# Cross-attention and expert FFN on one Trainium2 core: every moved probability tile turned by VectorE, four work banks, remainders and slot picks on GpSimd

## The chip, the cores and the metric

The kernel runs on one core of one Trainium2 chip. The metric is device time in microseconds (us) of one execution; a kernel's time is the median of several executions. The engines are TensorE (PE, with PEld for its weight loads), VectorE (DVE), ScalarE (ACT), GpSimd (POOL) and SyncE (SP), which here only issues transfers.

## The reference, cut to what matters

16 batches of 256 tokens, width 256, with a context of 256 rows of width 192; 16 heads of 64; then a top-2 router over 8 experts with a capacity of 640 rows each.

```python
x = x + attention(layernorm(x), ctx)       # w_q 256x1024, w_k and w_v 192x1024, w_o 1024x256
  sim = einsum('bhid,bhjd->bhij', q, k) * 64 ** -0.5
  out = einsum('bhij,bhjd->bhid', softmax(sim), v)
x = x + ffn(layernorm(x))                  # gates, top 2 of 8, capacity, gelu(buf @ w1 + b1) @ w2 + b2
```

All of it is in 32-bit floats. Most products are made of three: each operand is split into a rounded head (`qh`, `kh`, `ah`) and its remainder (`ql`, `kl`, `al`), and the product of two remainders is left out.

## The kernel before, in words

The attention part is cut into 64 periods, four to a batch; a period m handles four heads ("units" 0 to 3, two pairs `cc`). `timeline()` writes one list of stages, and each engine walks that list and runs its own stages in that order, so the order on every engine is fixed by hand. Semaphores join them. In period m:

- PE: `scores(m)` into banks 0 to 3, one bank for each unit; `pv(m-2)` (probabilities by values); `q(m+1)`, `k(m+1)`, `v(m)`; and by batch the output projection `o` (twice), the transposes `xt` and `x2t`, `logits` and `pos`.
- DVE: `max0` to `max3` (row maxima), `a_norm` (attended values by the inverse row sums), `inv` (reciprocals and their turn), the remainders `a_lo`, `q_lo`, `k_lo`, and router work.
- ACT: `exp0` to `exp3`, the heads `q_hi`, `k_hi`, `a_hi`, `v_sb`, and `copy2`, `copy3`.
- POOL: context splits (`ctx`), inverse roots, the residual with its bias, and `scatter` (four indirect transfers into the slot table).
- SP: `inv_out(m-1)`, `inv_in(m-1)`, `lift(m)`, `move(m)`, and once a batch `traffic`, which stores a batch and loads the next `x` and context.

The probabilities of a unit are 256x256 and have to be transposed before `pv`. Outside `MOVED` (periods 6 to 61, 56 of the 64) PE does it: four 128x128 transposes for each unit (`turn`), and ACT copies the result out of the bank. In `MOVED` PE turns units 2 and 3 alone (`by_pe`). Units 0 and 1 go another way: DVE turns every 32x32 square in place (`square0`, `square1`, L1279), `lift` writes the 512 KB of both units to memory (`squares`, L485), and `move` (L492) reads them back with the squares in transposed places, in four transfers, one for each group of 32 partitions.

`move(m)` waits on SP until `lift(m)` has landed. The inverse row sums make a like round: `inv_out` (L466) writes 128 partitions of 32 values to the table `inverses`, `inv_in` (L475) waits until that has landed and reads them back spread over 64 partitions, twice. All of this is one queue in one order:

```python
sp.wait_ge(sem("inv_out"), 16 * (m + 1))                # inv_in(m)
sp.wait_ge(sem("square"), 2 * (m - MOVED[0] + 1))       # lift(m)
sp.wait_ge(sem("lifted"), 16 * (m - MOVED[0] + 1))      # move(m)
sp.dma_start(inv_table[m % 2].rearrange("j (a i) -> a j i", a=GROUPS), invturned[:, m % 2, :])
```

`pv(m)` waits for `moved`. Products of `xt`, `q`, `k`, `v`, `pv`, `o`, `x2t` and `pos` take banks 5, 6, 7 in turn (`WORK_BANKS = 3`); each waits until the product three places before has been read. Bank 4 holds a turn of PE or the logits.

Of the kernel before, what the change touches and what calls it, by code (L numbers as in the profile page):

```python
# [19 lines left out]
F32 = mybir.dt.float32  # L20
# [44 lines left out]
MOVED = range(6, PERIODS - 2)  # L65
SQ = 32
# [3 lines left out]
def by_pe(m):  # L70

    return (2, 3) if m in MOVED else (0, 1, 2, 3)

# [11 lines left out]
def timeline():  # L85
# [12 lines left out]
    for m in range(1, PERIODS - 2):  # L98
# [4 lines left out]
        out += [("scores", m)] + ([("pv", m - 2)] if m >= 2 else [])  # L103
        out += [("logits", b - 2)] if r == 3 and 2 <= b else []
        if four:
            out += [("q", m + 1), ("turn0", m - 1), ("k", m + 1), ("turn1", m - 1), ("v", m), ("turn2", m - 1)]
        else:
            out += [("q", m + 1), ("turn2", m - 1), ("k", m + 1), ("turn3", m - 1), ("v", m)]
# [12 lines left out]
        out += steps("exp0 exp1", m) + ([("a_hi", m - 2)] if m >= 2 else []) + [("q_hi", m + 1)]  # L121
        if four:
            out += [("copy0", m - 1), ("exp2", m), ("k_hi", m + 1), ("copy1", m - 1), ("exp3", m), ("copy2", m - 1),
                    ("v_sb", m)]
        else:
            out += [("copy2", m - 1), ("k_hi", m + 1), ("exp2", m), ("copy3", m - 1), ("exp3", m), ("v_sb", m)]
# [9 lines left out]
        out += ([("a_norm", m - 2)] if m >= 2 else []) + [("inv", m - 1)]  # L136
        out += [("slot", b - 3)] if r == 2 and 3 <= b else []
        out += [("bias", b - 2)] if r == 3 and 2 <= b else []
        out += [("ln1_stats", 1)] if m == 1 else []
        out += ([("a_lo", m - 2)] if m >= 2 else []) + [("q_lo", m + 1)]  # L140
        out += [("square0", m)] if m in MOVED else []
        out += [("k_lo", m + 1)]
        out += [("square1", m)] if m in MOVED else []
        if r == 0:
            out += steps("shift compare rank gate", b - 3) if 3 <= b else []
            out += [("ln1", b + 1)] if 1 <= b < B - 1 else []
# [3 lines left out]
        if r == 2:  # L150
            out += steps("ln1 xt_lo", 1) if b == 0 else []
            out += [("ln2", b - 2)] if 2 <= b else []
            out += [("ln1_stats", b + 2)] if b + 2 < B else []
            out += [("keys", b - 3)] if 3 <= b else []
            out += [("x2add", ST * (b - 1))] if 1 <= b else []
        out += [("pick", b - 3)] if r == 3 and 3 <= b else []
# [5 lines left out]
                5: [("vsplit", 3)]}.get(m, [])  # L162
        out += [("scatter", b - 4)] if r == 0 and 4 <= b else []
# [5 lines left out]
        out += [("load_ctx", 3)] if m == 2 else []  # L169
        out += steps("inv_out inv_in", m - 1) + (steps("lift move", m) if m in MOVED else [])  # L170
        out += {2: steps("clear", 0), 3: steps("clear", 1), 4: steps("clear", 2)}.get(m, [])
        out += [("traffic", b - 2)] if r == 1 and 2 <= b else []
# [4 lines left out]
    out += [("scores", m), ("pv", m - 2), ("q", z), ("turn2", m - 1), ("k", z), ("turn3", m - 1), ("v", m),  # L177
# [5 lines left out]
    out += [*steps("exp0 exp1", m), ("q_hi", z), ("a_hi", m - 2), ("copy2", m - 1), ("k_hi", z), ("exp2", m),  # L183
            ("copy3", m - 1), ("exp3", m), ("v_sb", m), ("x2t_sb", c), ("w_hi", 0), ("w_hi", 1),
# [5 lines left out]
    out += [*steps("max0 max1 max2 max3", m), ("inv", m - 1), ("slot", c - 1), ("a_norm", m - 2), ("q_lo", z),  # L190
            ("a_lo", m - 2), ("k_lo", z), ("ln2", c), *steps("keys pick", c - 1), ("x2add", ST * d), ("inv", m),
# [16 lines left out]
def w_piece(w, cut):  # L208
# [6 lines left out]
WORK_BANKS = 3  # L215
# [5 lines left out]
APART = {**{("logits", b): 4 for b in range(B - 3)}, ("x2t", B - 2): 2, ("logits", B - 2): 3, ("pos", B - 2): 4, ("logits", B - 1): 4}  # L221
# [7 lines left out]
WORK_READ = {"xt": "xt_lo", "q": "q_lo", "k": "k_lo", "v": "v_sb", "pv": "a_lo", "o": "x2", "x2t": "x2t_sb",  # L229
             "logits": "biased", "pos": "slots"}  # L230


def build(nc, x, ctxt, wq, wk, wv, wo, bo, rw, rb, w1, b1, w2, b2, out):
    es = ExitStack()
    with es:
# [12 lines left out]
        square_table = nc.dram_tensor("squares", [2, P, 2 * ST * S], F32, kind="Internal").ap()  # L248
# [15 lines left out]
        invrows = sb(rest, "invrows", [2, S])  # L264
        xth, xtl = (sb(rest, n, [2, DC, S], F32R) for n in ("xth", "xtl"))
        c0 = sb(rest, "c0", [2, S])
        c1 = sb(rest, "c1", [2, S])
# [73 lines left out]
        def prob_pair(m):  # L341
            return flat(prob[:, m % 2, 0:2, :, :, :])

        def probt_pair(m):
            return flat(probt[:, m % 2, 0:2, :, :])
# [54 lines left out]
        def _(sp):  # L400
# [6 lines left out]
            def load_ctx(b):  # L407
                if b >= 2:
                    sp.wait_ge(sem("ctx"), b - 1)
                cols = slice(b * S, (b + 1) * S)  # L410
                sp.dma_start(c0[:, b % 2, :], ctxt[0:P, cols]).then_inc(sem(f"ctx_in{b % 2}"), 16)
                for h in range(2):
                    sp.dma_start(c1[h * HD:(h + 1) * HD, b % 2, :], ctxt[P:CD, cols])\
                      .then_inc(sem(f"ctx_in{b % 2}"), 16)
# [38 lines left out]
            load_ctx(2)  # L453

# [25 lines left out]
            def lift(m):  # L480
# [81 lines left out]
        def _(pool):  # L562
# [20 lines left out]
            def ctx(b):  # L583

                p = b % 2
                pool.wait_ge(sem(f"ctx_in{p}"), 48 * (b // 2 + 1))
# [3 lines left out]
                link(pool.tensor_copy(c1s[0:HD, p, :], c1[0:HD, p, :]))  # L590
                link(pool.tensor_copy(c1t[HD:P, :], c1[HD:P, p, :]))
                link(pool.tensor_copy(c0h[:, p, :], c0[:, p, :]))
                link(pool.tensor_tensor(c1s[HD:P, p, :], c1[HD:P, p, :], c1t[HD:P, :].bitcast(F32), ALU.subtract))
                link_as("ctx", pool.tensor_tensor(c0l[:, p, :], c0[:, p, :], c0h[:, p, :].bitcast(F32),
                                                  ALU.subtract))

            def inverse_root(which, n):
# [13 lines left out]
                link_as(f"{which}_rstd", pool.tensor_tensor(root, root, newton[:, :], ALU.mult))  # L611

# [44 lines left out]
            def slots(b):  # L657
# [6 lines left out]
                if b < B - 4:  # L664
                    pool.wait_ge(sem("q"), PER_B * (b + 4) + 2)
# [8 lines left out]
            for stage, n in TIMELINE:  # L674
# [9 lines left out]
                if stage in ("ln1_root", "ln2_root"):  # L684
                    inverse_root(stage[:3], n)
                if stage == "vsplit":
# [27 lines left out]
        def _(pe):  # L714
            work = {w: n for n, w in enumerate(WORKS)}

            def bank(stage, n):

                if stage == "logits" and n < B - 3:
                    pe.wait_ge(sem("probt"), turns_to(PER_B * (n + 2) + 1, UNITS - 1))  # L720
                    return psum[:, APART[stage, n], :]
# [4 lines left out]
                at = work[stage, n]  # L726
                if at >= WORK_BANKS:
                    s, m = WORKS[at - WORK_BANKS]
                    pe.wait_ge(sem(WORK_READ[s]), m + 1)
                return psum[:, 5 + at % WORK_BANKS, :]  # L730

# [74 lines left out]
            def turn(m, u):  # L806

                if u == 0 and m >= 1:
                    pe.wait_ge(sem("probt"), turns_to(m - 1, 3))
                if u in (1, 2) and m + 1 < PERIODS:  # L810
                    pe.wait_ge(sem("exp"), UNITS * (m + 1) + u)
                if u == 3:
                    pe.wait_ge(sem("probt"), turns_to(m, 0))
                    if m % PER_B == 2 and 2 <= m // PER_B < B - 1:
                        pe.wait_ge(sem("biased"), m // PER_B - 1)
# [7 lines left out]
            def pv(m):  # L823
# [7 lines left out]
                for cc in range(2):  # L831
                    for kb in range(ST):
                        for h in range(2):
                            cols = slice((2 * (c + cc) + h) * HD, (2 * (c + cc) + h + 1) * HD)
                            if m in MOVED and cc == 0:
                                p = probt_pair(m).rearrange("p (a u k q i) -> p u k q a i", a=GROUPS, u=2, k=ST, q=ST)[:, h, kb]
# [5 lines left out]
            def o(n, chunks=range(PAIRS)):  # L842

                b, t = divmod(n, ST)
                dst = bank("o", n) if chunks[0] == 0 else psum[:, 5 + work["o", n] % WORK_BANKS, :]
# [160 lines left out]
        def _(act):  # L1006
            copy = lambda dst, src, **kw: act.activation(dst, src, ACT.Copy, **kw)  # L1007
            def work_bank(stage, n):
                if (stage, n) in APART:
                    return psum[:, APART[stage, n], :]  # L1010
                return psum[:, 5 + WORKS.index((stage, n)) % WORK_BANKS, :]
# [38 lines left out]
            def exps(m, u):  # L1050
# [5 lines left out]
                if m >= 2 and u in by_pe(m - 2):  # L1056
                    act.wait_ge(sem("turn"), turns_to(m - 2, u))
                elif m >= 2:
                    act.wait_ge(sem(f"moved{m % 2}"), 16 * moves_to(m - 2))
                for qb in range(ST):  # L1060
                    into, out_of = prob[:, m % 2, u, :, qb, :], psum[:, u, qb * S:(qb + 1) * S]
                    if m in MOVED and u not in by_pe(m):
                        into = prob_pair(m).rearrange("p (g u k q j) -> p u q k g j", g=GROUPS, u=2, k=ST, q=ST)[:, u, qb]
# [17 lines left out]
            def pv(m):  # L1081
# [6 lines left out]
                copy(ah[:, b % 2, c:c + 2, :], work_bank("pv", m).rearrange("p (c s) -> p c s", c=2))\  # L1088
# [97 lines left out]
        def _(dve):  # L1186
# [7 lines left out]
            def work_bank(stage, n):  # L1194
                if (stage, n) in APART:
                    return psum[:, APART[stage, n], :]
                return psum[:, 5 + WORKS.index((stage, n)) % WORK_BANKS, :]
# [71 lines left out]
            def a_norm(m):  # L1269
# [3 lines left out]
                at = work_bank("pv", m).rearrange("p (c s) -> p c s", c=2)  # L1273
                dve.tensor_tensor(at, at, invrows[:, :, :], ALU.mult).then_inc(sem("a_norm"), 1)  # L1274

            def square(m, u):
# [278 lines left out]
```

## Time and profile before

| | us |
|---|---|
| median of 3 runs | 954.8 (954.76 to 957.25) |
| the profiled execution | 957.82 |
| its span | 956.1 |
| PE busy | 918.1 (96%) |
| DVE busy | 739.8 (77%) |
| ACT busy | 573.8 (60%) |
| POOL busy | 280.2 (29%) |
| DMA moved | 133.29 MB, 139 GB/s on average |

The span runs from the first to the last instruction of the profiled execution; its time is 1.7 us longer. A busy engine is not always the one that sets the end: the waits in front of it say so. SP has no busy time in the page; what it does is in its own timeline.

### The profile page before, as it was taken

Reading aid. Unit: us, or ns where it says so; the run is one execution under the profiler, and the core shown is the slowest. Engines: PE = TensorE matmul, PEld = TensorE weight load, DVE = VectorE, ACT = ScalarE, POOL = GpSimd, SP = SyncE. Lnnn points to the kernel's source line nnn. Section 1 sums busy time; section 2 is a strip of 40 time slices with the busy share of each in tenths; the row PEclk is TensorE's granted clock in tenths of the full one; section 3 lists DMA queues with packets and bytes.
Section 4 is the critical chain, followed back from the end, with each engine's and each line's share of the span. In section 5 each row is a group of like instructions: output and inputs, shape, how many; then the busy total and the mean of one; then the engine's idle time right before and its main releaser. Section 6 shows DMA issues by size and latency. Waiting matters only on the chain.

```text
span 956.1 us, 22462 instructions
## 1 busy us (share of the span) xinstructions
PE 918.1 (96%) x7916; PEld 821.0 (86%) x7916; DVE 739.8 (77%) x1745; ACT 573.8 (60%) x1600; POOL 280.2 (29%) x441
## 2 busy tenths in 40 slices
PE   7999999999999999999999999999889999999995
PEld 7878888888888888888888888888689999999995
DVE  5757778888888888888888888877777877678762
ACT  5877766667667666766766677676534433334420
POOL 5541112314233231323223132302533223322233
PEclk9999999999999999999999999999899999999999
DMA  8462535445455445455444445444345765645422
GB/s 239 143 205 91 163 123 163 162 152 168 146 157 158 148 157 164 136 172 164 139 156 161 146 130 170 136 134 136 121 133 99 149 145 123 135 84 98 112 29 27
DMA packets 152991, 133.29 MB, mean 139 GB/s; under 512 B 62140, under 2 KB 141610, under 8 KB 152752
## 3 DMA queue, kind: packets, MB, share of 16 engines
q1 hardware_dynamic: 144048, 122.87, 42.9%
q0 software_dynamic: 8832, 8.98, 5.4%
q8 instruction: 64, 1.05, 0.5%
q14 instruction: 47, 0.39, 0.1%
HBM read 82.15 MB, written 54.61 MB: 143 GB/s over the span
## 4 chain that ended last, share of the span: by engine, by line
PE 70%; DVE 11%; ACT 10%; issue 4%; DMA 3%; POOL 0%; SPq 0%; POOLq 0%; ACTq 0%; DVEq 0%
PE psum L734 20%; PE psum L839 9%; PE psum L996 9%; PE psum L855 9%; PE psum L980 8%; PE psum L801 7%; ACT prob L1067 6%; PE psum L819 5%; DVE negmax L1255 3%; DVE hidl L1201 2%; DVE bufl L1201 1%; ACT probt L1007 1%; DVE hidh L1488 1%; PE psum L879 1%; DVE psum L1274 1%
## 5 line engine op out<-in xcount | busy, mean ns | idle before, releaser
L1067 ACT ACTIVATE prob<-psum,negmax 128x256 f32<-128x256 f32 x512 | 238.0, 481 | 79.5 <-DVE negmax L1255 79.4
L1255 DVE TENSOR_REDUCE negmax<-psum 128x2 f32<-128x512 f32 x256 | 160.4, 682 | 29.7 <-PE psum L801 29.7
L1173 ACT ACTIVATE hid<-psum,b1t 128x640 f32<-128x640 f32 x64 | 50.9, 795 | 126.6 <-PE psum L980 125.0
L839 PE MATMUL psum<-probt,v 128*64 128x256 f32 x1024 | 124.6, 385 | 0.0
L707 POOL DMA_INDIRECT out_rows<-y,rowi x40 | 66.3, 1658 | 160.8 <-DVE y L1498 154.2
L1067 ACT ACTIVATION_READ_ACCUMULATOR prob<-psum,negmax 128x1 f32 x512 | 109.5, 214 | 0.0
L839 PEld LDWEIGHTS psum<-probt,v 128*64 128x64 f32 x1024 | 67.8, 136 | 36.4 <-issue 0.3
L668 POOL DMA_INDIRECT slot_table<-row,picki x64 | 66.8, 1044 | 96.9 <-PE psum L734 61.2
L996 PE MATMUL psum<-w2h,hidh 128*128 128x256 f32 x320 | 91.4, 286 | 2.9 <-DVE y L1498 1.5
L801 PE MATMUL psum<-kh,qh 64*128 64x256 f32 x512 | 82.5, 316 | 11.1 <-ACT prob L1067 8.9
L996 PE MATMUL psum<-w2l,hidh 128*128 128x256 f32 x320 | 90.5, 283 | 0.0
L996 PE MATMUL psum<-w2h,hidl 128*128 128x256 f32 x320 | 90.5, 283 | 0.0
L1007 ACT ACTIVATE probt<-psum 128x512 f32<-128x512 f32 x144 | 87.3, 609 | 4.4 <-PE psum L819 4.4
L819 PE MATMUL psum<-ident,prob 128*128 128x128 f32 x576 | 87.1, 276 | 2.7 <-ACT prob L1067 2.7
L734 PE MATMUL psum<-xth,wqh 128*128 128x256 f32 x256 | 78.9, 308 | 0.5 <-DVE xtl L1201 0.5
L1279 DVE STREAM_TRANSPOSE prob<-prob 128x512 f32<-128x512 f32 x112 | 78.6, 702 | 0.0
L855 PE MATMUL psum<-woh,ah 128*128 128x256 f32 x256 | 72.9, 285 | 1.6 <-DVE al L1201 1.6
L606 POOL TENSOR_SCALAR shifted<-ln_mean_var 128x2 f32<-128x2 f32 x32 | 7.1, 223 | 225.0 <-issue 182.7
L801 PE MATMUL psum<-kl,qh 64*128 64x256 f32 x512 | 72.9, 278 | 0.0
L801 PEld LDWEIGHTS psum<-kh,qh 64*128 64x128 f32 x512 | 48.8, 185 | 27.9 <-ACT prob L1067 13.3
L801 PE MATMUL psum<-kh,ql 64*128 64x256 f32 x512 | 72.8, 277 | 0.0
L855 PE MATMUL psum<-wol,ah 128*128 128x256 f32 x256 | 72.4, 283 | 0.0
(199 smaller groups left out, 2704.6 us busy)
## 6 DMA issues: line engine op xcount, KB each, us to landing
squares<-prob SPq DMA_DIRECT2D x56, 512.0 KB
probt<-squares SPq DMA_DIRECT2D x224, 128.0 KB, 2.8
invrows<-inverses SPq DMA_DIRECT2D x128, 128.0 KB
w1r<-in_w SPq DMA_DIRECT2D x8, 1024.0 KB
w2r<-in_w SPq DMA_DIRECT2D x8, 1024.0 KB, 9.1
slot_table<-blank SPq DMA_DIRECT2D x8, 662.5 KB, 6.5
blocks<-slot_table SPq DMA_DIRECT2D x56, 80.0 KB
xin<-in_x SPq DMA_DIRECT2D x16, 256.0 KB, 3.5
```

The lines of the kernel that those rows point to most:

```text
L668: pool.indirect_dma_start(out=table, out_offset=bass.IndirectOffsetOnAxis(ap=picki[:, b % 3, k, t:t + 1], axis=0), in_=row[:, b % 3, t, :] ...
L734: mm = pe.matmul(dst, lhs, rhs, start=(j == 0), stop=(j == len(terms) - 1))
L801: mm = pe.matmul(psum[:, 2 * cc + h, qb * S:(qb + 1) * S], a[r, m % 2, cc, cols], w[r, m % 2, cc, :], start=(j == 0), stop=(j == len(terms ...
L819: mm = pe.transpose(psum[:, TURN_BANK[u], kb * S + qb * P:kb * S + (qb + 1) * P], prob[:, m % 2, u, kb, qb, :], ident[:, :])
L839: mm = pe.matmul(dst[h * HD:(h + 1) * HD, cc * S:(cc + 1) * S], v[:, b % 2, kb, cols], p, start=(kb == 0), stop=(kb == ST - 1))
L855: mm = pe.matmul(dst[:, 0:D], a[:, b % 2, c, tt], w[:, c, :], start=(c == 0 and j == 0), stop=(c == PAIRS - 1 and j == 2))
L980: mm = pe.matmul(dst, lhs, rhs, start=(n == 0), stop=(n == len(terms) - 1))
L996: mm = pe.matmul(dst, a[:, j, ss], w[:, j, :], start=(j == 0 and m == 0), stop=(j == HC - 1 and m == 2))
L1007: copy = lambda dst, src, **kw: act.activation(dst, src, ACT.Copy, **kw)
L1067: last = act.activation(into, out_of, ACT.Exp, bias=negmax[:, m % 2, u, qb:qb + 1], accum_out=total[:, m % 2, u, qb:qb + 1])
L1255: dve.tensor_reduce(negmax[:, m % 2, u, :], psum[:, u, :].rearrange("p (q s) -> p q s", q=ST), AX.X, ALU.max, negate=True).then_inc(sem("m ...
L1279: dve.transpose(at, at).then_inc(sem("square"), 1)
```

## The change

1. In `MOVED`, `by_pe` is empty: PE turns nothing and ACT copies nothing. DVE turns the squares of all four units, in two instructions of 128x1024 (pairs of units) where there were two of 128x512.
2. `lift` writes all four units, 1 MB. `move` reads them back in four transfers again, now one for each group `a` of 32 source rows, each into all 128 partitions.
3. Bank 4 joins the work banks from period 6 on until period 62 (`places()`), also for the logits.
4. `pv(m-2)` comes after `q` and `k` in PE's period. `a_norm` writes to a new SBUF tile `attended` instead of back to its bank, and comes after `q_lo`, `square0`, `k_lo`; `a_hi` and `a_lo` read `attended`.
5. To POOL go `a_lo` of periods 4 to 59, `ln1` of batches 2 to 15, and the last steps of the slot picks (`pick_`, ranked by a subtraction); DVE keeps the two reductions (`extremes`).
6. On SP, `traffic` comes between `inv_out` and `inv_in`. The context tiles `c0`, `c1` have one buffer, and `scatter` starts after a `k` instead of a `q`.

```diff
 def by_pe(m):
-    return (2, 3) if m in MOVED else (0, 1, 2, 3)
+    return () if m in MOVED else (0, 1, 2, 3)
...
-            out += [("q", m + 1), ("turn2", m - 1), ("k", m + 1), ("turn3", m - 1), ("v", m)]
+            out += [("scores", m)] + ([("logits", b - 2)] if r == 3 and 2 <= b else [])
+            out += [("q", m + 1), ("k", m + 1), ("pv", m - 2), ("v", m)]
...
-            out += [("copy2", m - 1), ("k_hi", m + 1), ("exp2", m), ("copy3", m - 1), ("exp3", m), ("v_sb", m)]
+            out += [*steps("exp0 exp1", m), ("q_hi", m + 1), ("exp2", m), ("k_hi", m + 1), ("exp3", m),
+                    ("a_hi", m - 2), ("v_sb", m)]
...
+            out += [("inv", m - 1)] + ([("slot", b - 3)] if r == 2 and 3 <= b else [])
+            out += [("bias", b - 2)] if r == 3 and 2 <= b else []
+            out += [("q_lo", m + 1), ("square0", m), ("k_lo", m + 1), ("a_norm", m - 2)]
         out += [("square1", m)] if m in MOVED else []
...
-        out += steps("inv_out inv_in", m - 1) + (steps("lift move", m) if m in MOVED else [])
+        out += [("inv_out", m - 1)] + ([("traffic", b - 2)] if r == 1 and 2 <= b else [])
+        out += [("inv_in", m - 1)] + (steps("lift move", m) if m in MOVED else [])
...
-                sp.dma_start(square_table[m % 2], prob_pair(m)).then_inc(sem("lifted"), 16)
+                sp.dma_start(square_table[m % 2], prob_all(m)).then_inc(sem("lifted"), 16)
...
-                for g in range(GROUPS):
-                    sp.dma_start(probt_pair(m)[g * SQ:(g + 1) * SQ, :].rearrange("j (a c) -> j a c", a=GROUPS),
-                                 square_table[m % 2].rearrange("(a j) (g c) -> g j a c", a=GROUPS, g=GROUPS)[g])\
+                for a in range(GROUPS):
+                    sp.dma_start(probt_all(m).rearrange("p (a c) -> p a c", a=GROUPS)[:, a, :],
+                                 square_table[m % 2].rearrange("(a j) (g c) -> a g j c", a=GROUPS, g=GROUPS)[a])\
                       .then_inc(sem(f"moved{m % 2}"), 16)
...
+            def a_lo(m):
+                b, c = divmod(2 * m, PAIRS)
+                pool.wait_ge(sem("a_hi"), m + 1)
...
+                pool.tensor_tensor(al[:, b % 2, c:c + 2, :], attended[:, :, :],
+                                   ah[:, b % 2, c:c + 2, :].bitcast(F32), ALU.subtract).then_inc(sem("a_lo"), 1)
...
-                dve.tensor_tensor(at, at, invrows[:, :, :], ALU.mult).then_inc(sem("a_norm"), 1)
...
+                dve.tensor_tensor(attended[:, :, :], work_bank("pv", m).rearrange("p (c s) -> p c s", c=2),
+                                  invrows[:, :, :], ALU.mult).then_inc(sem("a_norm"), 1)
+
+            def square(m, pair):
+
+                dve.wait_ge(sem("exp"), UNITS * m + 2 * pair + 2)
+                at = prob_all(m).rearrange("p (g v c) -> p v g c", g=GROUPS, v=2)[:, pair]
                 dve.transpose(at, at).then_inc(sem("square"), 1)
```

## Rows read from the trace of the kernel before

**Rows 1.** The page: span and busy time of each engine.
```profile
span 956.1 us, 22462 instructions
PE 918.1 (96%) x7916; PEld 821.0 (86%) x7916; DVE 739.8 (77%) x1745; ACT 573.8 (60%) x1600; POOL 280.2 (29%) x441
```

**Rows 2.** One batch: us, busy of PE, PEld, DVE, ACT, POOL; clock, DMA share, GB/s.
```profile
389.06:431.10 42.04, 41.30 (x380) 35.58 (x379) 35.35 (x93) 29.11 (x92) 11.68 (x23) 1.00 0.48 154
```

**Rows 3.** The chain that ended last, 389 to 431 us: start, us, what.
```profile
391.32 0.44 PE psum L819 x4
```

**Rows 4.** Groups by shape, window 389.06 to 431.10: busy, mean ns, idle before.
```profile
L1279 DVE STREAM_TRANSPOSE prob<-prob 128x512 f32<-128x512 f32 x8 | 5.6, 702 | 0.0
...
L1007 ACT ACTIVATE probt<-psum 128x512 f32<-128x512 f32 x8 | 4.8, 601 | 0.0
...
L1201 DVE TENSOR_TENSOR al<-psum,ah 128x512 fp32r<-128x512 f32 x4 | 2.8, 692 | 1.1 <-ACT ah L1007 1.1
```

**Rows 5.** Groups by shape, whole span: the nearest rows for new shapes.
```profile
L1217 DVE TENSOR_SCALAR turning<-xin,ln_mean_var,ln_rstd 128x256 f32<-128x256 f32 x32 | 12.0, 418 | 2.6 <-POOL ln_rstd L611 2.3 <-issue 0.3
L1470 DVE STREAM_TRANSPOSE turned<-blocks 128x640 f32<-128x640 f32 x14 | 11.6, 834 | 0.0
...
L594 POOL TENSOR_TENSOR c0l<-c,c0h 128x256 fp32r<-128x256 f32 x16 | 12.2, 762 | 1.3
...
L617 POOL TENSOR_TENSOR wol<-wo_raw,woh 128x1024 fp32r<-128x1024 f32 x2 | 4.8, 2378 | 0.2
```

**Rows 6.** SP's timeline over one batch: start, us, issue.
```profile
389.06 1.75 SPq L492 DMA_DIRECT2D probt<-squares  x4
...
399.88 1.74 SPq L492 DMA_DIRECT2D probt<-squares  x4
401.66 0.57 SPq L466 DMA_DIRECT2D inverses<-invturned  x1
404.05 1.24 SPq L475 DMA_DIRECT2D invrows<-inverses  x2
405.39 0.54 SPq L485 DMA_DIRECT2D squares<-prob  x1
408.86 1.73 SPq L492 DMA_DIRECT2D probt<-squares  x4
...
413.85 0.58 SPq L466 DMA_DIRECT2D inverses<-invturned  x1
416.26 1.28 SPq L475 DMA_DIRECT2D invrows<-inverses  x2
...
421.35 1.75 SPq L492 DMA_DIRECT2D probt<-squares  x4
...
430.56 1.73 SPq L492 DMA_DIRECT2D probt<-squares  x4
```

**Rows 7.** SP's waits, window 78 to 663: us in total, times, longest.
```profile
SPq L492 <- DMA squares<-prob: 174.1, 56, 4.8
SPq L475 <- DMA inverses<-invturned: 78.6, 46, 2.5
SPq L466 <- DVE invturned L1267: 13.9, 12, 3.0
SPq L485 <- DVE prob L1279: 11.1, 17, 1.3
```

**Rows 8.** DMA, window 637.20 to 638.90, one `lift` alone: packets, share.
```profile
DMA packets 144, 0.52 MB, mean 308 GB/s; under 512 B 16, under 2 KB 16, under 8 KB 144
...
q1 hardware_dynamic: 144, 0.52, 76.2%
```

**Rows 9.** DMA, window 611.90 to 612.50, one `inv_out` alone.
```profile
DMA packets 132, 0.02 MB, mean 27 GB/s; under 512 B 132, under 2 KB 132, under 8 KB 132
...
q1 hardware_dynamic: 132, 0.02, 17.9%
```

**Rows 10.** DMA, window 401.75 to 402.75, in the middle of a `move`.
```profile
q1 hardware_dynamic: 299, 0.27, 88.0%
```

More of the change, by code:

```diff
@@ L65 @@
 MOVED = range(6, PERIODS - 2)
+POOL_REST = range(PER_B, PERIODS - 4)
 SQ = 32
@@ L135, in timeline @@
         out += ([("split_lo", 5)] if m == 1 else []) + steps("max2 max3", m)
[L136 to L142, printed above, removed]
+        if four:
+            out += ([("a_norm", m - 2)] if m >= 2 else []) + [("inv", m - 1)]
+            out += [("ln1_stats", 1)] if m == 1 else []
+            out += ([("a_lo", m - 2)] if 0 <= m - 2 < POOL_REST[0] else []) + [("q_lo", m + 1)]
+            out += [("square0", m)] if m in MOVED else []
+            out += [("k_lo", m + 1)]
+        else:
+            out += [("inv", m - 1)] + ([("slot", b - 3)] if r == 2 and 3 <= b else [])
+            out += [("bias", b - 2)] if r == 3 and 2 <= b else []
+            out += [("q_lo", m + 1), ("square0", m), ("k_lo", m + 1), ("a_norm", m - 2)]
         out += [("square1", m)] if m in MOVED else []
@@ L162, in timeline @@
                 5: [("vsplit", 3)]}.get(m, [])
+        out += [("ln1", b + 1)] if r == 0 and 1 <= b < B - 1 else []
         out += [("scatter", b - 4)] if r == 0 and 4 <= b else []
@@ L228, with places @@
 WORKS = [w for w in WORKS if w not in APART]
-WORK_READ = {"xt": "xt_lo", "q": "q_lo", "k": "k_lo", "v": "v_sb", "pv": "a_lo", "o": "x2", "x2t": "x2t_sb",
+WORK_READ = {"xt": "xt_lo", "q": "q_lo", "k": "k_lo", "v": "v_sb", "pv": "a_norm", "o": "x2", "x2t": "x2t_sb",
              "logits": "biased", "pos": "slots"}
+def places():
+    banks, last, found = [5, 6, 7], {}, {}
+    for stage, n in TIMELINE:
+        work = stage.removesuffix("_most"), n
+        if (stage, n) == ("turn0", PERIODS - 2):
+            banks.remove(4)
+            found[stage, n] = 4, last[4]
+        if work in WORKS and work not in found:
+            at = banks.pop(0)
+            banks.append(at)
+            found[work] = at, last.get(at)
+            last[at] = work
+        if (stage, n) == ("turn3", MOVED[0] - 1):
+            banks.append(4)
+    return found
+PLACES = places()
 def build(nc, x, ctxt, wq, wk, wv, wo, bo, rw, rb, w1, b1, w2, b2, out):
@@ L611, in inverse_root, with ln1, pick_ @@
                 link_as(f"{which}_rstd", pool.tensor_tensor(root, root, newton[:, :], ALU.mult))
+            def ln1(b):
+                pool.wait_ge(sem("xt"), b)
+                if b >= XRING:
+                    pool.wait_ge(sem("logits"), b - XRING + 1)
+                for t in range(ST):
+                    last = pool.tensor_scalar(xn[:, t, :], xin[:, b % XRING, t, :], mean_var["ln1"][:, t, 0:1],
+                                              rstd["ln1"][:, t:t + 1], ALU.subtract, ALU.mult)
+                last.then_inc(sem("ln1"), 1)
+            def a_lo(m):
+                b, c = divmod(2 * m, PAIRS)
+                pool.wait_ge(sem("a_hi"), m + 1)
+                if m == POOL_REST[0]:
+                    pool.wait_ge(sem("a_lo"), m)
+                    pool.wait_ge(sem("table_clear"), 16 * NE)
+                    pool.wait_ge(sem("spare_clear"), 16)
+                pool.tensor_tensor(al[:, b % 2, c:c + 2, :], attended[:, :, :],
+                                   ah[:, b % 2, c:c + 2, :].bitcast(F32), ALU.subtract).then_inc(sem("a_lo"), 1)
+            def pick_(b):
+                pool.wait_ge(sem("extremes"), b + 1)
+                if b >= 3:
+                    pool.wait_ge(sem(f"scatter{b % 3}"), 16 * 2 * ST * (b // 3))
+                pool.tensor_scalar(pick[:, 0, :], pick[:, 0, :], BIG, None, ALU.add)
+                link(pool.tensor_scalar(pick[:, 1, :], pick[:, 1, :], -1.0, None, ALU.add))
+                link(pool.tensor_tensor(same[:, 0, :], pick[:, 1, :], pick[:, 0, :], ALU.subtract))
+                link(pool.tensor_scalar(same[:, 0, :], same[:, 0, :], 0.0, BIG, ALU.is_le, ALU.mult))
+                link(pool.tensor_tensor(pick[:, 1, :], pick[:, 1, :], same[:, 0, :], ALU.add))
+                pool.tensor_copy(picki[:, b % 3, :, :], pick[:, :, :]).then_inc(sem("picks"), 1)
             def vsplit(w):
@@ L685, in _ @@
                     inverse_root(stage[:3], n)
+                if stage == "ln1" and n >= 2:
+                    ln1(n)
+                if stage == "a_lo" and n in POOL_REST:
+                    a_lo(n)
+                if stage == "pick" and n < B - 4:
+                    pick_(n)
                 if stage == "vsplit":
@@ L725, in bank @@
                     return psum[:, APART[stage, n], :]
[L726 to L730, printed above, removed]
+                at, user = PLACES[stage, n]
+                if user:
+                    pe.wait_ge(sem(WORK_READ[user[0]]), user[1] + 1)
+                elif at == 4:
+                    pe.wait_ge(sem("probt"), turns_to(MOVED[0] - 1, UNITS - 1))
+                return psum[:, at, :]
             def products(dst, terms):
@@ L1453, in _ @@
             for stage, n in TIMELINE:
-                if stage in steps:
+                if stage in steps and not (stage == "ln1" and n >= 2 or stage == "a_lo" and n in POOL_REST
+                                               or stage == "pick" and n < B - 4):
                     steps[stage](n)
```

121 lines of the change are left out of this document (60 added, 61 removed).

## The prediction

> **What bounds the kernel now.** I read the page first, then one batch by stretches, then the chain, then SP. The page gives PE 96% of the span and DVE 77% [rows 1]. The stretch of one batch says where that matters: PE is busy 41.30 of 42.04 us, DVE 35.35, ACT 29.11, POOL 11.68, at the full granted clock [rows 2]. The chain runs through PE for nearly all of the batch, the turns of PE included, 0.44 us each [rows 3]. So far PE is the bound.
>
> A second loop is nearly as long, and no busy column shows it. SP works in strict order: `move` waits for `lift` to land, and `inv_in` for `inv_out`. The starts of five successive `move`s lie 10.82, 8.98, 12.49 and 9.21 us apart, 41.50 in all, for a batch of 42.04 [rows 6]; the 12.49 has `traffic` in it. Of its waits between 78 and 663 us, 174.1 us are for a `lift` to land and 78.6 us for an `inv_out`. DVE kept SP waiting for 13.9 and 11.1 us in all, 25 us over 14 batches, or 1.8 us a batch [rows 7]. That is all the slack SP has. Any microsecond the change puts between one `move` and the next, beyond 1.8 a batch, lengthens the kernel, whatever PE gives back.
>
> **The change part by part.**
>
> *PE and ACT.* Eight turns of PE go from each batch: 8 x 0.44 = 3.5 us [rows 3]. With the 0.74 us in which PE is idle now [rows 2], a batch could fall to 37.8 us. ACT loses eight copies, 4.8 us [rows 4]; it is not the bound.
>
> *DVE.* There is no 128x1024 transpose in the trace. 128x512 takes 0.702 us [rows 4], 128x640 takes 0.834 [rows 5], so 1.03 ns for each further element and 1.23 us for 1024; its bounds are 0.83 and 1.40 (two of 0.702). I take 1.23: +8 x 0.53 = +4.2 us a batch (+1.0 to +5.6). It gives up four `a_lo` of 0.69 (2.8 us) [rows 4], two tensor_scalar of 0.42 (0.8 us) [rows 5], and the tail of a pick, five small instructions that I put at 0.5 to 1 us, by the 0.2 to 0.4 of the small rows. DVE ends near 35.2 us a batch, about what it has.
>
> *POOL.* A 128x512 subtraction lies between 0.76 (128x256) and 2.38 us (128x1024) [rows 5]; on the line between, 1.30. Four of them, two `ln1` instructions of 0.4 to 0.8 and a pick make about 8 us: 20 of 42. Hidden behind PE or DVE, with `a_lo` a whole period ahead of the next `a_norm`; if that cover failed it would cost DVE up to 1.3 us a period.
>
> *Banks, orders, context.* Four banks, `pv` after `k`, and one context buffer move waits, not work. Cost nothing: `pv(m)` now comes some 3 us later in its period, which covers late transfers; the context load still has about three periods.
>
> *lift.* A `lift` alone is 144 packets: 128 of data and 16 small ones that signal [rows 8]. 76.2% of 1.7 us on 16 engines is 20.7 us, so 161 ns for each 4 KB packet, eight to an engine. Twice the bytes: +8 x 0.161 = +1.3 us until it lands, for each period. `move` waits for it, so all of it is on SP's path: +5.2 us a batch.
>
> *move.* This decides. Before, both sides of each of its four transfers have 32 rows outermost. Now the destination has 128 partitions outermost, and the source `(g j) c` has 4 blocks of 32 rows. The trace has one transfer with such a pair of sides, in the other direction: `inv_out`, 128 partitions to a table walked 4 x 32. It shows 132 packets, 128 of data and 4 that signal, where a `lift` has 16 [rows 8, 9]. Its share is 17.9% of 0.6 us on 16 engines, 1.72 us or 13 ns a packet, and `lift` fills three quarters of the engines' time where this fills a sixth. I read that as four engines instead of 16, one for each block of the outer 4, and expect the same when the 4 is on the source side. The profile doesn't show which engines; as all `inv_out`s and `move`s would be of one kind, I take the same four.
>
> The price then: 4 transfers x 128 packets of 2 KB on 4 engines are 128 packets for each. A packet of 2 KB lies on the line between 13 ns (128 B) and 161 ns (4 KB): 85 ns, bounds 80 (half of 161) and 94 (two of a `move` of now, 88.0% x 1 us x 16 / 299 packets = 47 ns) [rows 8 to 10]. 128 x 85 ns = 10.8 us (10.2 to 12.0).
>
> The Trainium skill, DMA: Bandwidth & Descriptors, section "Why a DMA increments its semaphore by 16 and not by 1", says that a transfer takes the largest number of engines up to 16 that divides the outermost size of both sides, and the lowest-numbered ones. By that rule the new `move` takes four, always the same, and the sum is the one below; were the count set by the destination alone, it would be the 16-engine rival. The trace agrees for a destination of 4 (the four signals of rows 9); for a source of 4 no run here shows it.
>
> *inv_out behind move.* Now it is issued 1.78 us after `move` starts, and `inv_in` at +4.17 (404.05 - 399.88) [rows 6]. Of that, move's own data are 512 x 47 ns / 16 engines at 88% [rows 10], 1.7 us; 2.5 us are the start, inv_out's own data and its landing. With 10.8 us of data on four engines, and `inv_out` queued behind them on the same four, `inv_in` starts at +13.3: 9.1 more in each of the three periods without `traffic`. In the period with it, `inv_in` started at +7.4 (416.26 - 408.86); it is +5.9 there, and I take 1 (0 to 2) for traffic's data, which now lie in front of the lift.
>
> *The sum.* 41.5 + 3 x 9.1 + 5.9 + 1 + 5.2 = 80.9 us for four periods; less the waits on DVE, which vanish (1.8), 79.1. That is 37 us more than 42.04, over 56 moved periods or 14 batches: +519 us. The profiled execution takes 957.8, so 1477; the median is 3 us lower than that execution: 1474, say **1470 us**. A packet of 80 or 94 ns moves it by -36 or +65 us, the term for `traffic` by 14 either way, the bounds of the lift by little. I put this case's own range at 1400 to 1540.
>
> **Rivals.**
>
> 1. *All 16 engines carry the move, SP still the bound (0.24).* Then a `move` has 32 packets of 85 ns for each engine instead of 32 of 47: +1.2 us. `inv_out`'s signal comes 0.6 to 1.1 later, +2.4 us for three periods; `traffic` between saves 1.6 in the fourth; `lift` +5.2. 41.5 + 2.4 - 1.6 + 5.2 = 47.5 a batch, 45.7 less the slack of 1.8: +3.7 to +5.5, +52 to +77 us, so 1005 to 1030; 1015 is its price, and some 980 if transfers overlap better than that. For it: only the source has the 4. Against it: the pair of sides is that of `inv_out` mirrored.
>
> 2. *The other sign: SP's loop isn't lengthened and PE is paid (0.13).* Place: SP between `lift` and the next `lift`. It decides if the doubled transfers add less than 1.8 us a batch, where I count at least 5.2 for `lift` alone. Then PE's 37.8 us holds, -4.2 x 14 = -59 us at most, some of it lost to DVE at 93% of that: 900 to 920. For it: DMA is busy 48% on average [rows 2], and `pv` has 3 us more grace. Against it: average share says nothing of a queue that waits for each landing.
>
> 3. *DVE becomes the bound in its own order (0.05, with what is not foreseen).* Its 35.2 us is in order behind waits on `pv`, ACT and now POOL; 1.3 us for each period would bring 42 again: 950 to 975.
>
> **How the numbers follow.** The four-engine move gets 0.58. Its mechanism rests on one row of the mirrored kind, which is why it isn't more. The predicted time is its own, 1470. The range must reach to the 16-engine case, so it is 980 to 1545: 0.55 of the first, 0.23 of the second. Differences of 0.3% are about what a measurement of this kernel can tell from none. Faster 0.13 (rival 2); same 0.03 (part of rival 3); slower 0.84.
>
> **What would show it.** In the profile after: `move` starts some 19 to 20 us apart; a single `move` transfer with 4 signalling packets, 132 in place of 144; DMA share near a quarter for 10 us of each period; `inv_in` 13 us behind `move`; PE and DVE both half idle, PE's wait on `probt` before `pv`. Right for 16 engines: intervals near 11.5 us, 144 packets a transfer. Wrong on both counts: PE still 98% busy in a batch of 38 us. If the four transfers used four different sets of engines, they would run side by side in 3 us and the result would be rival 1's. No turn of PE (L819) should be left between 90 and 650 us, and DVE's two transposes should take 1.2 us each.

## The result: 1491 us, 56% slower

| | us |
|---|---|
| before, median of 4 runs | 955.65 (954.76 to 957.25) |
| changed, median of 4 runs | 1491.01 (1486.35 to 1493.18) |
| ratio | 1.559 (95%: 1.555 to 1.564) |

The page of the changed kernel: busy time and share of each engine, then the granted clock in 40 slices, and the chain that ended last.

```profile
span 1491.4 us, 21278 instructions
PE 987.3 (66%) x7468; PEld 835.7 (56%) x7468; DVE 744.5 (50%) x1601; ACT 516.7 (35%) x1488; POOL 401.2 (27%) x597
...
PEclk9997777888777787777888787778777779999999
...
DMA 55%; PE 22%; SPq 8%; DVE 8%; issue 3%; ACT 2%; POOLq 0%; POOL 0%; ACTq 0%; DVEq 0%
DMA inverses<-invturned 29%; DMA probt<-squares 14%; DMA squares<-prob 12%; PE psum L1056 6%; PE psum L1040 6%; PE psum L899 5%; SPq L517 5%; SPq L500 3%; DVE negmax L1316 2%; PE psum L792 2%; PE psum L859 1%; DVE hidl L1262 1%; ACT prob L1128 1%; DVE prob L1343 1%; DVE bufl L1262 1%
```

No engine is busy for more than two thirds of the span, where PE had 96% [rows 1]. The chain is 55% DMA, and its first entry is a table of 16 KB, the inverse sums. SP's timeline over two periods (start, us, issue) shows why:

```profile
608.66 2.45 SPq L517 DMA_DIRECT2D probt<-squares  x4
611.15 1.48 SPq L491 DMA_DIRECT2D inverses<-invturned  x1
...
622.23 1.26 SPq L500 DMA_DIRECT2D invrows<-inverses  x2
623.60 0.54 SPq L510 DMA_DIRECT2D squares<-prob  x1
628.42 2.44 SPq L517 DMA_DIRECT2D probt<-squares  x4
630.91 1.53 SPq L491 DMA_DIRECT2D inverses<-invturned  x1
641.18 1.25 SPq L500 DMA_DIRECT2D invrows<-inverses  x2
...
647.38 2.50 SPq L517 DMA_DIRECT2D probt<-squares  x4
```

The `move`s start 19.8 and 19.0 us apart, where they had 9 to 12.5 [rows 6]. `inv_in` starts 13.6 us behind `move` with `traffic` and 12.8 without; it was 4.2 without. The DMA packets from the start of a `move` to `inv_in` (628.42 to 641.20):

```profile
DMA packets 661, 1.08 MB, mean 85 GB/s; under 512 B 148, under 2 KB 148, under 8 KB 660
```

148 small packets are the 128 of `inv_out` and 20 that signal: four for each of five transfers. `inv_out` alone had 4 and `lift` 16 [rows 8, 9]. In the middle of the `move` (631.00 to 639.50):

```profile
DMA packets 432, 0.86 MB, mean 101 GB/s; under 512 B 12, under 2 KB 12, under 8 KB 432
...
q1 hardware_dynamic: 432, 0.86, 26.1%
```

For 8.5 us the share is 26.1%, four engines of 16 with nothing between packets: 26.1% x 8.5 x 16 / 420 data packets = 84.5 ns each. Had the four transfers used different sets of engines, they would have run side by side and the share would have been up to four times that. Which four engines they are, no run shows.

SP's waits between the first and the last `move` (window 83 to 1194: us, times, longest), to be read against [rows 7], which cover the same 56 `move`s:

```profile
SPq L500 <- DMA inverses<-invturned: 420.9, 55, 11.2
SPq L517 <- DMA squares<-prob: 237.6, 56, 6.0
SPq L491 <- DVE invturned L1328: 15.1, 17, 1.6
```

The wait for the inverses, and the 29% that the chain gives them, is not the time of 16 KB: `inv_out` is issued at 630.91, and the `move` in front of it has landed only at 640.85.

### The profile page after: what moved, and what is told of

Same layout as the page of the kernel before. It is cut to its first block, busy times and chain, and to the rows that moved or that the text cites. A ratio compares the mean times of both kernels' runs of the same rounds, so it can differ in the third digit from the quotient of the medians.

```text
span 1491.4 us, 21278 instructions
## 1 busy us (share of the span) xinstructions
PE 987.3 (66%) x7468; PEld 835.7 (56%) x7468; DVE 744.5 (50%) x1601; ACT 516.7 (35%) x1488; POOL 401.2 (27%) x597
## 4 chain that ended last, share of the span: by engine, by line
DMA 55%; PE 22%; SPq 8%; DVE 8%; issue 3%; ACT 2%; POOLq 0%; POOL 0%; ACTq 0%; DVEq 0%
DMA inverses<-invturned 29%; DMA probt<-squares 14%; DMA squares<-prob 12%; PE psum L1056 6%; PE psum L1040 6%; PE psum L899 5%; SPq L517 5%; SPq L500 3%; DVE negmax L1316 2%; PE psum L792 2%; PE psum L859 1%; DVE hidl L1262 1%; ACT prob L1128 1%; DVE prob L1343 1%; DVE bufl L1262 1%
## 5 line engine op out<-in xcount | busy, mean ns | idle before, releaser
L899 PE MATMUL psum<-probt,v 128*64 128x256 f32 x1024 | 218.1, 599 | 476.6 <-DMA probt<-squares 476.6
L899 PEld LDWEIGHTS psum<-probt,v 128*64 128x64 f32 x1024 | 115.9, 212 | 544.7 <-issue 540.5
L1336 DVE TENSOR_TENSOR attended<-psum,invrows 128x512 f32<-128x512 f32 x64 | 44.2, 691 | 579.6 <-PE psum L899 482.5
L1128 ACT ACTIVATE prob<-psum,negmax 128x256 f32<-128x256 f32 x512 | 240.5, 489 | 95.7 <-DVE negmax L1316 93.9
L1067 ACT ACTIVATE ah<-attended 128x512 fp32r<-128x512 f32 x64 | 40.5, 632 | 622.2 <-DVE attended L1336 622.2
L654 POOL TENSOR_TENSOR al<-attended,ah 128x512 fp32r<-128x512 f32 x56 | 72.3, 1291 | 246.7 <-ACT ah L1067 244.5
L1343 DVE STREAM_TRANSPOSE prob<-prob 128x1024 f32<-128x1024 f32 x112 | 138.3, 1234 | 0.7 <-ACT prob L1128 0.7
L1128 ACT ACTIVATION_READ_ACCUMULATOR prob<-psum,negmax 128x1 f32 x512 | 113.4, 222 | 0.0
L859 PE MATMUL psum<-kh,qh 64*128 64x256 f32 x512 | 79.5, 305 | 4.3 <-ACT probt L1067 2.3
L915 PE MATMUL psum<-woh,al 128*128 128x256 f32 x256 | 72.3, 282 | 0.0
```

What stands on the lines that cost most here:

```text
L654: pool.tensor_tensor(al[:, b % 2, c:c + 2, :], attended[:, :, :], ah[:, b % 2, c:c + 2, :].bitcast(F32), ALU.subtract).then_inc(sem("a_lo" ...
L859: mm = pe.matmul(psum[:, 2 * cc + h, qb * S:(qb + 1) * S], a[r, m % 2, cc, cols], w[r, m % 2, cc, :], start=(j == 0), stop=(j == len(terms ...
L899: mm = pe.matmul(dst[h * HD:(h + 1) * HD, cc * S:(cc + 1) * S], v[:, b % 2, kb, cols], p, start=(kb == 0), stop=(kb == ST - 1))
L915: mm = pe.matmul(dst[:, 0:D], a[:, b % 2, c, tt], w[:, c, :], start=(c == 0 and j == 0), stop=(c == PAIRS - 1 and j == 2))
L1128: last = act.activation(into, out_of, ACT.Exp, bias=negmax[:, m % 2, u, qb:qb + 1], accum_out=total[:, m % 2, u, qb:qb + 1])
L1343: dve.transpose(at, at).then_inc(sem("square"), 1)
```

## The experiments

A table first; the interval is (last minus first start of a `move` transfer) / 55, from the view of the tile `squares` (in e6 of SP's half). Each ratio is to the kernel before as it was timed beside that run (medians 956.0 to 957.3). e7 and e8 leave the exchange of the squares out, so `pv` gets misplaced probabilities; all other kernels compute the reference.

| label | base and edit | us (median) | ratio (95%) | interval, us |
|---|---|---|---|---|
| | before | 955.65 | | 10.57 |
| | changed | 1491.01 | 1.559 (1.555 to 1.564) | 20.17 |
| e1_by_g | changed, move by destination group | 1139.1 | 1.192 (1.185 to 1.199) | 13.82 |
| e2_before_by_a | before, move by source group | 1170.5 | 1.223 (1.218 to 1.228) | 14.40 |
| e3_by_g_sp | e1, new SP order | 976.1 | 1.020 (1.017 to 1.023) | 10.81 |
| e4_by_a_sp | changed, new SP order | 1316.9 | 1.376 (1.370 to 1.382) | 16.96 |
| e5_before_sp | before, new SP order | 960.3 | 1.004 (1.002 to 1.006) | 10.67 |
| e6_two_queues | e3, half of move from ScalarE | 958.1 | 1.001 (0.999 to 1.003) | 10.52 |
| e7_straight | changed, squares not exchanged | 1062.3 | 1.110 (1.107 to 1.114) | 12.54 |
| e8_straight_sp | e7, new SP order | 932.2 | 0.975 (0.972 to 0.978) | 10.03 |
| e9_strided_keys | changed, 128 outermost by key order | 1060.7 | 1.109 (1.106 to 1.112) | 12.38 |
| e10_strided_keys_sp | e9, new SP order | 932.6 | 0.975 (0.972 to 0.977) | 10.01 |
| e11_a_lo_early | e10, a_lo ahead of scatter | 910.8 | 0.952 (0.950 to 0.954) | 9.68 |

### Is it the number of engines, or the doubled bytes?

e1_by_g undoes one statement of the change; e2_before_by_a does it alone in the kernel before (there with `probt_pair` and half the bytes).

```diff
-                for a in range(GROUPS):
-                    sp.dma_start(probt_all(m).rearrange("p (a c) -> p a c", a=GROUPS)[:, a, :],
-                                 square_table[m % 2].rearrange("(a j) (g c) -> a g j c", a=GROUPS, g=GROUPS)[a])\
+                for g in range(GROUPS):
+                    sp.dma_start(probt_all(m)[g * SQ:(g + 1) * SQ, :].rearrange("j (a c) -> j a c", a=GROUPS),
+                                 square_table[m % 2].rearrange("(a j) (g c) -> g j a c", a=GROUPS, g=GROUPS)[g])\
```

> The changed kernel with its four move transfers cut by destination group again (32 partitions from 32 rows, both sides 32 outermost), the same bytes in the same 2 KB packets. Theory A (the outer 4 of the source confines each transfer to four engines): every transfer signals with 16 packets, a move's data take 32 x 85 ns = 2.7 us instead of 10.8, move starts come about 11.5 us apart, and the kernel takes 1005 to 1030 us, still over the kernel before because SP's loop lift, move, inv_out, inv_in is longer than 10.5 us. Rival B (the doubled bytes, or rows of the table read 8 KB apart, are slow on any engines): stays above 1300. Rival C (SP's loop isn't the second bound): 900 to 930.

> The kernel before with only its move transfers cut by source row group, into all 128 partitions (source 4 blocks of 32 rows outermost), 1 KB packets, same bytes. Theory A: 4 signals for each transfer, 128 packets x 47 ns = 6.0 us of data on four engines instead of 1.7 us on 16; inv_in starts 4.3 us later in three periods, some 2.5 in the one with traffic, less 1.8 of slack: +13.6 us a batch, +190 us, about 1145 (1090 to 1190). Rival B (doubled bytes were the cost): 956, no change.

e1: 1139, so 352 of the 535 us are this one statement; e2: 1170, +215 us with not a byte more, inside its range. Its packets from a `move` to `inv_in` (426.51 to 434.84) are 512, 128 and 20 that signal, four for each transfer, as in the changed kernel:

```profile
DMA packets 660, 0.54 MB, mean 65 GB/s; under 512 B 148, under 2 KB 660, under 8 KB 660
```

In e1 the packets from a `move` to `inv_in` (401.30 to 408.40) are 708: 512, 128 and 68 that signal, 16 for each of four transfers and 4 for `inv_out`.

```profile
DMA packets 708, 1.07 MB, mean 150 GB/s; under 512 B 196, under 2 KB 196, under 8 KB 708
```

The outer 4 on the source side gives four engines as it does on the destination side. But e1 is 110 us over what theory A said. Its packets explain part of that. In the middle of a `move` (404.50 to 407.00):

```profile
DMA packets 306, 0.55 MB, mean 220 GB/s; under 512 B 38, under 2 KB 38, under 8 KB 306
...
q1 hardware_dynamic: 306, 0.55, 104.5%
```

104.5% x 2.5 x 16 / 268 = 156 ns for 2 KB from start to end, where four engines took 84.5 (a share over 100% says that packets of one engine overlap a little). A transfer's 16 engines write to the same 32 partitions.

### Does the set of partitions matter, and what would a good transfer give?

e7_straight has 128 outermost on both sides:

```diff
-                                 square_table[m % 2].rearrange("(a j) (g c) -> a g j c", a=GROUPS, g=GROUPS)[a])\
+                                 square_table[m % 2].rearrange("p (a c) -> a p c", a=GROUPS)[a])\
```

> The changed kernel with each move transfer reading 512 columns of all 128 rows of the table into the 128 partitions in the same order: 128 outermost on both sides, the same bytes and 2 KB packets, but the squares don't change places, so pv gets wrongly placed probabilities. Theory P: 144 packets a transfer with 16 signals, 84 ns a packet, no port contention, a move's data in 2.7 to 3 us, move starts 11.5 us apart, 1005 to 1040, well under the 1139 of the kernel by destination group. If 2 KB packets are slow on 16 engines whatever the partitions: 1130 to 1150.

e9_strided_keys gets the same shape with the squares in the right places, by choosing which keys a square holds:

```diff
-                        out_of = out_of.rearrange("p (k g j) -> p k g j", k=ST, g=GROUPS)
+                        out_of = out_of.rearrange("p (k j g) -> p k g j", k=ST, g=GROUPS)
...
-                                 square_table[m % 2].rearrange("(a j) (g c) -> a g j c", a=GROUPS, g=GROUPS)[a])\
+                                 square_table[m % 2].rearrange("(a j) (g c) -> a (j g) c", a=GROUPS, g=GROUPS)[a])\
```

Square g now holds the keys 4j+g instead of 32g+j. Its row j goes to partition 4j+g, and the blocks for partitions 0, 1, 2, ... lie one behind the other in the table.

> The changed kernel, computing the reference again, with 128 rows outermost on both sides of a move: the exponentials read the scores of a unit with a step of four keys, so that square g holds the keys 4j+g, and the 128 blocks of 512 values that a move reads for the 128 partitions lie one behind the other in the table. SP's order as in the change. Theory A+P (16 engines, all ports): the time of e7, 1050 to 1075, and 16 signals a transfer. If the strided read of the scores costs ScalarE anything, ACTIVATE L1128 rises above its 489 ns.

1062 and 1061: they agree (22 us over e7's forecast, inside e9's), and are 77 and 78 us under e1 with as many engines and packets. Each transfer of e7 reads the same 128 pieces of the table as one of e1, and e9 reads others that lie one behind the other; e7 and e9 agree, so the source makes no visible difference, and the set of partitions is what is left. Against the changed kernel, whose transfers write all 128 partitions as well, e7 is 429 us faster by its one statement: that is the price of the four engines with the partitions kept. In e9 a `move` packet (422.00 to 424.00) takes 96.7% x 2 x 16 / 272 = 114 ns on average, between 156 and 84.5:

```profile
DMA packets 304, 0.57 MB, mean 287 GB/s; under 512 B 31, under 2 KB 31, under 8 KB 303
...
q1 hardware_dynamic: 303, 0.56, 96.7%
```

The average hides two kinds: by the trace's packet records for this window, 88% of the packets take 90 ns or less, as on four engines, and 6% take over 200. Over all `move`s the mean is 89 ns in the changed kernel, 104 in e9 and 144 in e1.

The Trainium skill, DMA: Bandwidth & Descriptors, section "Where 436 GB/s comes from", has 16 ports into SBUF. If 32 partitions reached only some of them, that would fit the 156 ns; no run separates the ports, so that mechanism is argued, not shown.

The strided read of the scores costs nothing that can be seen: the activation L1128 has a mean of 489 ns in e10, and 489 in the changed kernel.

### SP's order

The new order, first in four kernels; e5, whose base has `traffic` behind `move`, gets it in the same place:

```diff
-        out += [("inv_out", m - 1)] + ([("traffic", b - 2)] if r == 1 and 2 <= b else [])
-        out += [("inv_in", m - 1)] + (steps("lift move", m) if m in MOVED else [])
+        out += [("inv_out", m - 1)] + (steps("lift", m) if m in MOVED else []) + [("inv_in", m - 1)]
+        out += ([("traffic", b - 2)] if r == 1 and 2 <= b else []) + (steps("move", m) if m in MOVED else [])
```

> As the kernel with moves cut by destination group, and SP's order changed to inv_out, lift, inv_in, traffic, move, so that the landing of inv_out is no longer waited for between two moves and inv_in and traffic are issued while lift lands. Theory A: SP's loop falls to about lift to land 5.0 us + move 1.7 + inv_out 0.6 = 7.3 us, under PE's 9.5, and the batch goes to PE's 37.8 to 39 us: 900 to 925. Rival D (DVE, 35.2 us a batch with waits in fixed order, or late transfers for pv, bound it): 940 or more, with PE waiting on probt or on DVE.

> The changed kernel (moves by source row group, four engines) with the new SP order alone. Theory A: the four engines still carry 10.8 us of move, 2.6 of lift, 0.75 of inv_in and 0.4 of inv_out in each period, about 15 us, and a lift queues behind the move before it on them; the round trip of inv_out goes. Move starts 15 to 17 us apart, 1240 to 1340 us. If instead only the number of serial round trips counted and not the four engines' time, it would fall below 1150.

> The kernel before with only SP's order changed (inv_out, lift, inv_in, traffic, move). If SP's loop was a second bound close behind PE, as the slack of 1.8 us a batch says, but not the bound, then the kernel is PE's: 945 to 957, at most 1% faster. If SP's loop was what held it, 41.5 us would fall to about 30 and the batch to PE's busy 41.3: 10 us faster, 945. Slower than 960 would say that inv_in, now late in the period, holds a_norm.

> The straight read (squares not exchanged) with the new SP order. What the change could give if its transfers ran on 16 engines and 16 ports: SP's loop under 9 us, the batch at PE's 37.8 to 39, 900 to 925. If it stays at 950 or over, DVE (35.2 us a batch in fixed order) or late inverses hold it, and the whole way of turning on VectorE gives little.

e3: -163 us against e1; e4: -174 against the changed kernel; e8: -130 against e7. The serial round trips were a large part. e4's `move`s are 16.96 us apart, in the range that the four engines' own time gave (15 to 17), so their time is the rest.

e5 is the control, and it corrects the reading of the kernel before. SP's waits there (window 78 to 663), against [rows 7]:

```profile
SPq L485 <- DVE prob L1279: 174.8, 56, 3.9
SPq L466 <- DVE invturned L1267: 77.1, 42, 3.0
SPq L492 <- DMA squares<-prob: 47.3, 42, 1.8
SPq L475 <- DMA inverses<-invturned: 0.7, 1, 0.7
```

The waits for landings fell from 253 to 48 us and those for DVE rose from 25 to 252. SP got more than 200 us of slack, and the kernel got 0.4% slower. SP's loop had not bound the kernel before; PE, busy 98% of a batch [rows 2], did. The 4 us lost may come from `a_norm`, which now finds its inverses late more often (22.1 us in 24 waits of DVE in the view of the tile `invrows`; before it was 2.5 in 4); that this reaches PE isn't shown:

```profile
  DMA invrows<-inverses: 22.1, 24
```

e3 missed 900 to 925 by 51 us, e8 by 7. Between the two only the cut of `move` differs, and PE waited 31.1 us for `probt` in e3 and 0.2 in e8 (tile `squares`), so 44 of the 51 us are the transfers. SP still waited for landings in e3,

```profile
SPq L500 <- DMA inverses<-invturned: 201.6, 62, 5.6
SPq L517 <- DMA squares<-prob: 66.8, 44, 3.2
```

and a `lift` is now issued behind the `move` before it, whose packets take 144 ns on average. Feeding it from a second queue was e6:

```diff
-                for g in range(GROUPS):
+                for g in range(GROUPS // 2):
...
+            def move_more(m):
+                act.wait_ge(sem("lifted"), 16 * (m - MOVED[0] + 1))
+                act.wait_ge(sem("pv"), m - 1)
+                for g in range(GROUPS // 2, GROUPS):
+                    act.dma_start(probt_all(m)[g * SQ:(g + 1) * SQ, :].rearrange("j (a c) -> j a c", a=GROUPS),
+                                  square_table[m % 2].rearrange("(a j) (g c) -> g j a c", a=GROUPS, g=GROUPS)[g])\
+                       .then_inc(sem(f"moved{m % 2}"), 16)
```

> As e3 (moves by destination group, new SP order), but groups 2 and 3 of each move are issued by ScalarE after exp3 of the next period, so that two queues feed the engines. Theory P (a transfer into 32 partitions reaches only half of the ports, so 2 KB packets take 150 ns instead of 84 when 16 engines write to the same 32): with groups of both halves in flight some packets fall to 84 ns, less than e3: 930 to 965. If ScalarE's waits cost more than that gives: 980 or more.

958: 18 us under e3, in its range, and level with the kernel before. It helps, but it doesn't say whether by the packets' times or by SP's issues that went.

### The best version

> As e9 with the new SP order (inv_out, lift, inv_in, traffic, move). Theory A+P: the time of e8, 925 to 940, 2 to 3% under the kernel before, move starts 9 to 10 us apart, PE busy 96% of a batch.

932.6, as e8. Between 150 and 600 us its waits include these:

```profile
POOL xin L687 <- DMA slot_table<-row,picki: 35.8, 11, 4.5
DVE attended L1336 <- POOL al L654: 29.3, 11, 3.9
```

That is the moved `a_lo`: once a batch POOL, at the residual (L687), waits for the scatter to land, `a_lo` stands behind it, and DVE's next `a_norm` waits to overwrite `attended`. e11 puts `a_lo` first in that period:

```diff
+        out += [("a_lo", m - 2)] if m - 2 in POOL_REST and r == 0 else []
         out += [("scatter", b - 4)] if r == 0 and 4 <= b else []
...
-        out += [("a_lo", m - 2)] if m - 2 in POOL_REST else []
+        out += [("a_lo", m - 2)] if m - 2 in POOL_REST and r else []
```

> As e10, and a_lo on POOL stands in front of scatter and the residual in the first period of a batch, so that DVE's a_norm no longer waits for POOL, which waits for the scatter to land (28 us of such waits between 150 and 600 us in e8). If those waits reach PE: 5 to 20 us less than e10. If only DVE's idle time moves: the same as e10 within 0.3%.

910.8, 22 us under e10 (5 to 20 were expected) and 4.8% under the kernel before. Busy time in three stretches (PE, PEld, DVE, ACT, POOL; clock, DMA share, GB/s), e10 first:

```profile
200.00:300.00 100.00, 94.68 (x850) 79.20 (x850) 85.10 (x200) 61.68 (x207) 53.19 (x93) 1.00 0.78 264
300.00:400.00 100.00, 94.73 (x845) 79.25 (x842) 86.19 (x197) 62.04 (x207) 47.95 (x82) 1.00 0.78 262
400.00:500.00 100.00, 98.02 (x897) 82.27 (x896) 88.83 (x212) 63.14 (x211) 54.58 (x95) 1.00 0.81 274
```

```profile
200.00:300.00 100.00, 100.00 (x891) 83.74 (x891) 92.38 (x208) 65.21 (x222) 55.46 (x93) 1.00 0.83 280
300.00:400.00 100.00, 99.39 (x912) 83.58 (x911) 93.38 (x214) 65.66 (x217) 50.77 (x94) 1.00 0.84 282
400.00:500.00 100.00, 99.64 (x891) 83.34 (x891) 93.45 (x211) 65.88 (x222) 55.62 (x92) 1.00 0.81 269
```

PE is at 99.4 to 100%, where e10 had 94.7 to 98.0, now with the turns gone; DVE at 93% is close behind.

## Why the prediction was right

- *Four engines, always the same, for a source of 4 blocks.* Right: 20 signals for five transfers, share 26.1% with four transfers queued; e1 takes the effect away and e2 brings it about, each by one statement. This is the mechanism on which the time was forecast.
- *10.8 us of data, 85 ns a packet.* 84.5 ns; `move` started at 628.42, and `inv_in`, behind it and `inv_out`, at 641.18.
- *`inv_in` at +13.3.* 13.6 and 12.8, with `traffic` and without. *lift to move about 5 us* (3.7 on average before, and 1.3 more): 4.8 (628.42 - 623.60), 5.0 on average.
- *79.1 us for four periods.* 4 x 20.17 = 80.7. The term that was a little off is the packet: over all `move`s it takes 89 ns on average, not 85, which is 128 x 4 ns = 0.5 us of data. `inv_in` comes 13.73 us behind `move` on average over the 55 intervals, not 13.3, and four times that is 1.7 us. All the rest of the sum was put at 25.9 us (79.1 less 4 x 13.3) and came out at 25.8. From the first `move` to the last the kernel grew by 528 us (1109.5 against 581.3), outside them by 7, and the forecast had 519 for all of it. So the number is right for its own reasons. The step that nothing before had shown is the one under it, that a 4 on the source side does what a 4 on the destination side does; it held, and the forecast gave it 0.58.
- *The waits of SP on DVE, "which vanish".* 15.1 us in 17 waits are left, where [rows 7] have 25 in all, but they cost the loop nothing. By the records of the trace, `inv_out`'s issue ends at the latest 5.4 us behind the start of its `move`, and no `move`'s last data packet ends before 11.9: issued earlier, `inv_out` would only have stood longer behind the same four engines. The chain that ended last (start, us, what) puts such a time down to the small table:

```profile
630.16 10.69 DMA probt<-squares
...
649.92 11.72 DMA inverses<-invturned
```
- *A clock that no step of the sum had.* With PE waiting for a `move`, its granted clock goes from 1.00 to 0.50, the lower of its two levels (1.2 of 2.4 GHz). `pv` starts just then (at 640.98), and the clock is back at 1.00 by 646. A matmul of `pv` takes 599 ns, where it had 385. Three stretches (us, busy of each engine, then clock, DMA share, GB/s), and the group of `pv`:

```profile
637.00:639.00 2.00, 0.00 (x0) 0.00 (x0) 0.16 (x1) 0.02 (x1) 0.00 (x0) 1.00 0.26 102
639.00:641.00 2.00, 0.02 (x2) 0.05 (x2) 0.00 (x0) 0.00 (x0) 0.00 (x0) 0.50 0.21 71
641.00:645.00 4.00, 4.00 (x17) 2.28 (x18) 0.00 (x0) 0.00 (x0) 0.00 (x0) 0.50 0.49 180
```

```profile
L899 PE MATMUL psum<-probt,v 128*64 128x256 f32 x1024 | 218.1, 599 | 476.6 <-DMA probt<-squares 476.6
```

  The Trainium skill, TensorE: Matmul & The Clock Gate, section "Part 1: The HAM clock gate", has two states of that gate, 1.2 and 2.4 GHz; these rows show both. The slower `pv` cost SP's loop nothing that these waits show: between the first and the last `move` no `lift` waited for DVE's squares, and the waits for the inverses are those above.
- *DVE and POOL* (groups by shape). Right in size: a 128x1024 transpose 1.23 us (forecast 1.23), `a_lo` on POOL 1.29 (1.30). That DVE's busy time would stay about the same was right, too (744.5 us against 739.8).

```profile
L654 POOL TENSOR_TENSOR al<-attended,ah 128x512 fp32r<-128x512 f32 x56 | 72.3, 1291 | 246.7 <-ACT ah L1067 244.5
...
L1343 DVE STREAM_TRANSPOSE prob<-prob 128x1024 f32<-128x1024 f32 x112 | 138.3, 1234 | 0.7 <-ACT prob L1128 0.7
```

- *"A second loop is nearly as long", with 1.8 us a batch as all the slack.* Right for a change that lengthens the loop, and misleading for one that shortens it: e5 shows that it bound nothing.
- *Rival 1, 16 engines: 1005 to 1030.* It would have been 1061 (e9). The mis-sized term is the packet: 104 ns on average over all `move`s and 114 in the middle of one, not 85, when all 16 engines run. `inv_in` came 5.9 us behind `move` on average, where 4.2 and about 0.8 more were put. And with the destination cut as before it is 1139 (e1), where 2 KB packets into 32 partitions take 144 ns on average and 156 in the middle of a `move`.
- *Rival 2, 900 to 920.* The mechanism is real, but only with another order on SP and another shape of `move`: 911 in e11, with `a_lo` moved as well. There a batch is 3.6 us shorter than before (4 x (10.57 - 9.68)); 4.2 was the forecast for the turns and PE's idle time.
- *"`a_lo` a whole period ahead of the next `a_norm`", at no cost.* Wrong in one period of four. Behind the scatter it cost 22 us once the transfers no longer hid it (e10 to e11).

## What to carry to other kernels

Look at the outermost size of both sides of every transfer before its bytes: a reshape that reads well on the page can leave 12 of 16 engines idle, and whatever is issued behind it waits on the busy four. If a shuffle forces a small outer size, look for a freedom further up (here, which keys a square holds) that makes the blocks contiguous. Order a transfer queue so that nothing in it waits for a landing while something else could be issued, but don't take a nearly full queue for the bound: free it in an otherwise unchanged kernel first.

## What the runs showed that I had not expected

- The time of a 2 KB packet depends on the company. In the middle of a `move` it is 84.5 ns on four engines, 114 with 16 engines into 128 partitions, 156 with 16 into 32. The 114 is a mean of many packets at 84 and a few above 200; of the packets behind the 156, 97% take over 130 ns.
- A 32-bit activation that reads its bank with a step of four values takes the time of a contiguous one, 489 ns.
- `inv_out`'s own issue on SP grew from 0.57 us to between 1.5 and 2.0 behind a `move` on four engines, also where it waited for nothing from DVE (630.91 and 671.26 in SP's timeline). Behind a `move` on 16 engines it is 0.55 in e9, so it goes with the four busy engines.
